# Context projections and causal scores: a 64-row matmul tile against a full one half filled with zeros

## The reference

```
x   = x + xattn(layernorm(x), ctx)           # ctx: 77 x 192, 8 heads of 64
        q = x Wq ; k = ctx Wk ; v = ctx Wv    # Wk, Wv: 192 x 512
        out = softmax(q k^T / 8) v Wo + bo
x   = x + ffn(layernorm(x))                  # 16 experts, head size 64
        rw = gating(x)                        # 256 x 16
        q = sum_e rw[:,e] (x q_proj[e])       # 256 x 64, k and v alike
        scores = q k^T / 8, causal
        attn = softmax(scores) v
        out = sum_e (attn * rw[:,e]) o_proj[e]
```

## Time and profile before

| what | value |
|---|---|
| median of 3 runs (lowest, highest) | 2855.37 us (2851.93, 2856.12) |
| span of the profiled execution | 2854.2 us |
| the median less that span | 1.2 us |
| mean granted TensorE clock | 0.989 |
| TensorE matmul busy | 2764.7 us, 97% |
| TensorE weight load busy | 2594.7 us, 91% |
| VectorE busy | 2444.3 us, 86% |
| ScalarE busy | 1000.0 us, 35% |
| GpSimd busy | 1189.2 us, 42% |

### The profile page before, as it was taken

How to read it: one execution, slowest core, us unless ns; L and a number is a source line. 1 busy time by engine, 2 the same in 40 slices (tenths; PEclk the granted TensorE clock), 3 DMA queues, 4 the chain that set the end, 5 groups by cost and what they waited for, 6 DMA issues and landing times.

```text
span 2854.2 us, 64365 instructions
## 1 busy us (share of the span) xinstructions
PE 2764.7 (97%) x19012; PEld 2594.7 (91%) x19012; DVE 2444.3 (86%) x6754; ACT 1000.0 (35%) x2320; POOL 1189.2 (42%) x1739
## 2 busy tenths in 40 slices
PE   5999999999999999999999999999999999999997
PEld 4999999999999999999999999999999999999996
DVE  6888888888888888888888888888888888888885
ACT  3233333333333333333333333333333333333331
POOL 1343443434434434434434444344344344344343
PEclk7999999999999999999999999999999999999998
DMA  4111111111111111111111111111111111111111
GB/s 102 28 44 35 38 43 27 43 47 27 43 43 31 43 43 31 43 41 33 43 32 40 45 27 43 44 30 43 43 31 43 43 31 43 36 38 43 27 39 42
DMA packets 131435, 113.58 MB, mean 40 GB/s; under 512 B 24720, under 2 KB 130640, under 8 KB 131408
## 3 DMA queue, kind: packets, MB, share of 16 engines
q1 hardware_dynamic: 131408, 113.23, 16.2%
HBM read 95.38 MB, written 17.83 MB: 40 GB/s over the span
## 4 chain that ended last, share of the span: by engine, by line
PE 80%; DVE 11%; issue 7%; POOL 1%; DVEq 1%; ACT 1%; POOLq 0%; DMA 0%; SPq 0%
PE bank_b L372 10%; PE bank_b L373 9%; PE bank_b L374 9%; PE bank_a L372 8%; PE bank_a L374 8%; PE bank_a L373 8%; PE bank_c L372 4%; PE bank_c L374 4%; PE bank_c L373 4%; PE bank_a L484 4%; DVE acc L992 3%; DVE acc L989 2%; PE bank_a L444 2%; DVE mix L1033 1%; PE bank_a L415 1%
## 5 line engine op out<-in xcount | busy, mean ns | idle before, releaser
L372 PE MATMUL bank_b<-wqkv_hi,x2T_lo 128*128 128x384 f32 (+1 forms) x2048 | 726.2, 355 | 34.2 <-DVE acc L992 33.6
L373 PE MATMUL bank_b<-wqkv_lo,x2T_hi 128*128 128x384 f32 (+1 forms) x2048 | 693.5, 339 | 0.0
L374 PE MATMUL bank_b<-wqkv_hi,x2T_hi 128*128 128x384 f32 (+1 forms) x2048 | 689.0, 336 | 0.0
L992 DVE SCALAR_TENSOR_TENSOR acc<-bank_b,rw,acc 128x192 f32<-128x192 f32 x1792 | 641.4, 407 | 5.1 <-PE bank_b L374 2.6
L1248 POOL TENSOR_TENSOR mixs_lo<-mix,mixs_hi 128x512 fp32r<-128x512 f32 x256 | 379.9, 1513 | 153.9 <-ACT mixs_hi L769 153.9
L372 PEld LDWEIGHTS bank_b<-wqkv_hi,x2T_lo 128*128 128x128 f32 x2048 | 386.4, 189 | 57.5 <-DVE acc L992 53.4
L373 PEld LDWEIGHTS bank_b<-wqkv_lo,x2T_hi 128*128 128x128 f32 x2048 | 386.6, 189 | 0.0
L374 PEld LDWEIGHTS bank_b<-wqkv_hi,x2T_hi 128*128 128x128 f32 x2048 | 385.1, 188 | 0.0
L1170 POOL TENSOR_TENSOR pow_out<-pow_in,expo 128x2 f32<-128x2 f32 (+1 forms) x128 | 111.7, 873 | 600.0 <-DVE pow_in L849 512.8
L372 PE MATMUL bank_c<-wo_hi,mixs_lo 128*128 128x256 f32 x1024 | 293.8, 287 | 3.7 <-POOL mixs_lo L1248 3.7
L374 PE MATMUL bank_c<-wo_hi,mixs_hi 128*128 128x256 f32 x1024 | 287.8, 281 | 0.0
(11 more groups left out here) (193 smaller groups left out, 6990.9 us busy)
## 6 DMA issues: line engine op xcount, KB each, us to landing
rw_all<-rw_dram SPq DMA_DIRECT2D x128, 512.0 KB, 5.9
xt<-in_x_dram SPq DMA_DIRECT2D x64, 256.0 KB, 2.7
out_dram<-mix SPq DMA_DIRECT2D x64, 256.0 KB, 2.2
ct<-in_ctx_dram SPq DMA_DIRECT2D x64, 57.8 KB
ct<-in_ctx_dram SPq DMA_DIRECT2D x64, 19.2 KB
mix<-in_L_ffn_o_proj_dram SPq DMA_DIRECT2D x2, 512.0 KB, 4.3
rw_dram<-rwT SPq DMA_DIRECT2D x64, 16.0 KB, 1.4
x_tiles<-in_L_xattn_Wq_dram SPq DMA_DIRECT2D x1, 512.0 KB, 7.0
```

The source lines that it names most:

```text
L372: nc.tensor.matmul(dst, lhs[1], rhs[0], start=start, stop=False)
L373: nc.tensor.matmul(dst, lhs[0], rhs[1], start=False, stop=False)
L374: return nc.tensor.matmul(dst, lhs[0], rhs[0], start=False, stop=stop)
L992: V.scalar_tensor_tensor(acc[:, t, k, :], src, rw[:, t, e:e + 1], acc[:, t, k, :], ALU.mult, ALU.add).then_inc(b_evac, 1)
```

## The change

The last pass of the context projections and the second pass of the causal scores read all 128 rows. The high tile of the context's chunk 1 and a new tile `q_rows` have zeros in rows 64 to 127, so that these rows add nothing. `qk_hi` is replaced by `q_rows` (q, rows 0 to 63) and `k_hi` (k, rows 64 to 127). ScalarE makes three copies instead of two for the context and four instead of three for q and k. Two memsets at the start, on VectorE, are larger or new.

```diff
-        qk_hi = sb("qk_hi", [P, T], F32R)
+        k_hi = sb("k_hi", [P, T], F32R)
+        q_rows = sb("q_rows", [P, T], F32R)
...
-                return nc.tensor.matmul(dst, cT[0][0:D, 1, 0:NC], w_[0][0:D, 1, :], start=False, stop=True)
+                return nc.tensor.matmul(dst, cT[0][:, 1, 0:NC], w_[0][:, 1, :], start=False, stop=True)
...
-                    last = nc.tensor.matmul(dst, qk_hi[0:D, t * P:(t + 1) * P], k_stack[0:D, 0:keys], start=False, stop=True)
+                    last = nc.tensor.matmul(dst, q_rows[:, t * P:(t + 1) * P], k_stack[:, 0:keys], start=False, stop=True)
...
-                nc.scalar.activation(cT[0][:, :, 0:NC], src[:, :, 0:NC], copy)
+                nc.scalar.activation(cT[0][:, 0, 0:NC], src[:, 0, 0:NC], copy)
+                nc.scalar.activation(cT[0][0:D, 1, 0:NC], src[0:D, 1, 0:NC], copy)
...
-                nc.scalar.activation(qk_hi[:, :], src, copy)
+                nc.scalar.activation(q_rows[0:D, :], src[0:D, :], copy)
+                nc.scalar.activation(k_hi[D:P, :], src[D:P, :], copy)
...
-            for k in range(2):
-                V.memset(cT[k].bitcast(F32)[:, :, NC:NCE], 0.0).then_inc(pad_done, 1)
+            V.memset(cT[0].bitcast(F32)[:, :, :], 0.0).then_inc(pad_done, 1)
+            V.memset(cT[1].bitcast(F32)[:, :, NC:NCE], 0.0).then_inc(pad_done, 1)
...
+            V.memset(q_rows.bitcast(F32)[D:P, :], 0.0).then_inc(pad_done, 1)
...
-                for stack, rows in ((q_stack, slice(0, D)), (k_stack, slice(D, P))):
-                    last = V.tensor_tensor(stack[rows, :], bank_c(C_QK)[rows, 0:T], qk_hi.bitcast(F32)[rows, :], ALU.subtract)
+                for stack, hi, rows in ((q_stack, q_rows, slice(0, D)), (k_stack, k_hi, slice(D, P))):
+                    last = V.tensor_tensor(stack[rows, :], bank_c(C_QK)[rows, 0:T], hi.bitcast(F32)[rows, :], ALU.subtract)
```

## The result

| | median us | lowest, highest | ratio to before, 95% interval |
|---|---|---|---|
| before, same chip | 2855.74 | 2851.93, 2857.53 | |
| changed kernel | 2805.70 | 2802.43, 2807.78 | 0.9824 [0.9811, 0.9836] |

What follows compares the result with a forecast made beforehand. Bound by a loop: TensorE up to the first cross scores, then VectorE until it releases TensorE. Scores 0.08 earlier and 0.74 shorter give 0.82 a batch, 52 us over 64 batches: 2854.2 - 52 + 1.2 = 2803.4 us, range 2786 to 2828.

Steps and rivals of the forecast that it cites:

- The steps of the key projection: TensorE, end of the key product: steps 0.33 and 0.38 both become 0.23, four transposes 0.06 less; 0.31 us a product.
- GpSimd's sum: Holds the q and k transposes until 1407.71; TensorE could come at 1407.61; just fits, late it costs what exceeds 0.09.
- The score term: TensorE's causal scores: five steps shrink from 1.37 to 0.63 us, 0.74 saved a batch, bounds 0.57 to 0.82.
- The wait at k_stack: New TensorE idle ahead of the scores, released by VectorE's k_stack: some 0.3 to 0.45 us in each of 64 batches.
- The start of the scores: Value product's end 0.47 us earlier, ScalarE's added copy +0.39: scores start 0.08 earlier, though TensorE is there 0.62 earlier.
- The third copy for the context, put at nothing: ScalarE's added context copy, covered by two expert products on TensorE; uncovered at most 0.385 us a batch.
- the check that 0.74 had to fit into 1.02: VectorE, q_stack to row maximum: needs 0.74 us of idle to close, has 0.58, 0.18 and 0.26, 1.02 in all.
- the second rival (something else late): ScalarE's order, VectorE's idle times or GpSimd's sum limits the gain: 2813 to 2826 us, 13%.
- TensorE's wait for the accumulation: TensorE's wait for a VectorE accumulation, at 1424.61 in the kernel before: 0.55 us of idle, forecast to stay 0.55.
- TensorE's whole saving (2768): Rival: all of TensorE's saved time counts, 1.36 us a batch, 87 us in all: 2768 us, 6%.
- the paid copy without a head start (2833): Rival: value product ends no earlier and ScalarE's added copy is paid in full; 0.35 us a batch, 2833 us, 5%.
- the slower one: Rival: full-array loads still wait for the running matmul, and the added copy delays scores 0.39 us a batch: 2880 us, 3%.

Runs made afterwards that it cites:

- the run with the early q subtraction: Changed kernel with ScalarE copying q first and VectorE's q_stack subtraction released after the second copy instead of the fourth: 2783.23 us.
- The extra copy in its own run: Changed kernel with a fifth ScalarE copy of 64 rows, into rows of k_hi that nothing reads: 2829.78 us.
- the three faster versions: Changed kernel with q copied first and its subtraction released early (2783.23 us), without the copy to k_hi (2783.16 us), and with both edits (2781.34 us).

## Why the prediction was right

**TensorE's steps.** The steps of the key projection came as worked out: 0.33 and 0.38 became 0.23 and 0.22, the four transposes 0.44 instead of 0.50. Behind the value product only the first did: 0.33 became 0.24, and the 0.38 became 0.36, since GpSimd's sum held line 541; the forecast had allowed for that (its 1407.77). The score term was mis-sized: 0.68 us instead of 0.63. I had taken 0.12 for the third step, and it took 0.18. The load rows go with it: loads are 0.10 to 0.11 apart up to the fourth, so the load for the fourth pass starts at 1384.24, 0.05 after the start of the third pass. The next load starts together with the fourth pass, at 1384.37. The wait at k_stack is not the reason, for without it the step is as long (1455.79 to 1455.97 in the run with the early q subtraction). This is 0.05 x 64 = 3 us of the forecast.

**The start of the scores.** Measured from the fourth pass of the key product, the scores started 5.97 us later before (1404.90 to 1410.87) and 5.89 after (1378.03 to 1383.92): 0.08 earlier, as forecast. The value product ended earlier, the copies took 0.39 more, and VectorE's k_stack set the start. The extra copy in its own run gives that term by itself, 24 us for 64 copies.

**GpSimd's sum.** The transposes of line 541 now wait for it, with their weight load, in 60 batches, where before none of these loads did, and start 0.36 behind the last value pass. It cost nothing, since ScalarE's copy at 1381.43 follows v_hi without a wait and the scores waited anyway. The same 60 waits stand in the traces of the three faster versions, where TensorE's own arrival sets the start of the scores; what the sum costs there no run shows. The third copy for the context, put at nothing, shows no cost: TensorE waits for a context tile twice in the whole run, 10.3 us, as before (10.2).

**What reached the chain.** The row maximum stands 11.97 us behind the fourth pass before and 11.19 after, 0.78; the batch, first score pass to first score pass, takes 43.39 us before (the next one is at 1454.26) and 42.60 after. The medians over all batches are 43.36 and 42.61: 0.75, or 48 us for 64, where the forecast had 0.82. Most of the difference is the score term. The gain of 4.4 us ahead of the first scores, with the clock beside it, was not in the forecast, and 45.5 + 4.4 + 0.4 make up the 50. That 50 came so near to 52 is in part luck; the mechanism and its terms stand without it. The idle of 0.58 and 0.18 on VectorE was used up and the 0.26 kept, so the check that 0.74 had to fit into 1.02 was the right one, and the second rival (something else late) didn't come. TensorE's wait for the accumulation, 0.55 us ahead of 1396.96 in the changed kernel, is the 0.55 of the earlier trace rows, as the forecast had it. The other rivals fall with single runs: TensorE's whole saving (2768) with the scores alone, the paid copy without a head start (2833) with the projections alone, and the slower one with the load of line 445 at 1378.03 beside a matmul on the same 128 rows.

**The wait.** Its size was forecast as 0.3 to 0.45, in each of 64 batches; TensorE's matmuls show it in 60 of them. The row of the matmul has 0.16 and that of the load 0.31; by starts it is 0.59 - 0.23 = 0.36, the last from the run where nothing waits. A matmul's modelled end covers a part of the idle time.

## What to carry to other kernels

A single pass on half the rows between passes on all of them saved nothing here and cost 0.16 to 0.17 us at each change of rows: fill the rest of the stationary tile (the operand that is loaded as weights) with zeros, or put the half passes side by side. Before an edit that shortens one engine, look what the next step on it waits for: here the shorter steps were worth 1.3 us of TensorE a batch and the batch got 0.75 shorter, mostly since copies on an engine at 36% decided when the scores could start. The rest is then had by shortening that path, by ordering copies so that the second engine can start on half of them, or by leaving a copy out.

## What the runs showed of the hardware

- A change between a 128-row and a 64-row matmul costs 0.16 to 0.17 us, in two places and in a run that changed only their number. The loader does not run ahead over it: 0.41 us of idle before the 64-row load, none after the change. The Trainium skill's page TensorEngine Tiling (Array Packing), Tiling Modes, Key Properties, says that a change of tiling mode drains TensorE. The runs agree so far as they show the pause and its price, not a drain itself. The Trainium skill's page TensorE: Matmul & The Clock Gate, Part 3, The mechanism, says that a load overlaps matmuls only on other row groups. Taken alone this does not hold for line 445's load, which starts at 1378.03 with a matmul on the same 128 rows; the section also names a background weight buffer as a way for a load to go ahead, and no run here tells the two apart.
- Zeros in half of the stationary tile cost TensorE no time: the full pass of 512 columns takes 0.39 to 0.40 us as its neighbours do.
- VectorE's subtraction which reads its second operand in rows 0 to 63 and writes rows 64 to 127 takes 0.43 us for 64x256, the same as with all operands in the same rows.
